# Decoder layer on one core: queries and keys projected apart, scores as plain fp32 products on the two 64-row halves, loop reordered

## What is computed

```python
# x: 8 x 256 x 128, context: 8 x 512 x 128, fp32
x = x + attn(layernorm(x))        # rmsnorm * scale; 16 heads of 64; softmax(q k^T / 8) v; w_out, b_out
x = x + xattn(ctx, layernorm(x))  # one head of 128, 512 context rows, biases on q, v and output
x = x + ffn(layernorm(x))         # 128 -> 512 -> 128, relu, activations and weights quantised to 8 bit
```

```python
q = jnp.einsum('bsd,dhe->bshe', h, wq)
k = jnp.einsum('bsd,dhe->bshe', h, wk)
...
weights = jnp.einsum('bqhd,bkhd->bhqk', q, kf)
```

## Time and profile before

| | |
|---|---|
| runs | 435.38, 437.57, 438.6 us, median 437.57 |
| span of the profiled execution | 435.1 us |
| its own time | not listed apart; the three runs are from 0.3 to 3.5 us above this span |
| busy: TensorE, weight loads | 402.7 us (93%), 333.1 us (77%) |
| busy: VectorE, ScalarE, GpSimd | 322.4 us (74%), 262.0 us (60%), 161.5 us (37%) |
| chain that ended last | TensorE 65%, VectorE 18%, issue 8%, ScalarE 6% |

### The profile page before, as it was taken

One profiled execution on the slowest core, in us unless ns is written; L12 is line 12 of the kernel. 1 busy time (PEld: TensorE's weight loads), 2 busy tenths in 40 slices (PEclk: granted clock), 3 DMA queues, 4 the chain that ended last, 5 costly groups with the idle time before them and its releaser, 6 DMA issues.

```text
span 435.1 us, 9030 instructions
## 1 busy us (share of the span) xinstructions
PE 402.7 (93%) x2981; PEld 333.1 (77%) x2981; DVE 322.4 (74%) x780; ACT 262.0 (60%) x808; POOL 161.5 (37%) x177
## 2 busy tenths in 40 slices
PE   3889999999999999999999999999999999998646
PEld 3787888788878887888888887898788888866115
DVE  2677767866897489867886689748976779757883
ACT  2576665665566565575566556665566565825672
POOL 1055334542454344542454245434454244421000
PEclk9899999999999999999999999999999999999668
DMA  7400000000100010001000010001000000000003
GB/s 232 130 2 2 0 2 2 2 2 2 36 2 3 2 36 0 0 0 36 0 0 0 2 34 0 0 0 36 0 0 0 24 2 2 1 2 0 0 0 98
DMA packets 11878, 7.50 MB, mean 17 GB/s; under 512 B 1232, under 2 KB 11216, under 8 KB 11856
## 3 DMA queue, kind: packets, MB, share of 16 engines
q1 hardware_dynamic: 11568, 6.69, 5.2%
q10 hardware_dynamic: 288, 0.52, 0.4%
HBM read 6.16 MB, written 1.05 MB: 17 GB/s over the span
## 4 chain that ended last, share of the span: by engine, by line
PE 65%; DVE 18%; issue 8%; ACT 6%; DMA 1%; POOL 1%; DVEq 0%; POOLq 0%; ACTq 0%
PE o_bank L467 11%; PE pT L458 9%; PE acc_bank L474 7%; DVE negmax L897 5%; PE score L437 5%; PE score L435 5%; PE score L436 5%; ACT prob L731 4%; PE side_bank L435 3%; PE q_bank L435 2%; PE q_bank L437 2%; PE side_bank L437 2%; PE q_bank L436 2%; PE side_bank L436 2%; PE side_bank L512 2%
## 5 line engine op out<-in xcount | busy, mean ns | idle before, releaser
L1249 POOL TENSOR_TENSOR prob<-prob,rinv 128x512 f32<-128x512 f32 x128 | 133.0, 1042 | 200.6 <-DVE rinv L901 196.8
L731 ACT ACTIVATE prob<-score,negmax 128x256 f32<-128x256 f32 x256 | 118.9, 470 | 103.3 <-DVE negmax L897 103.2
L897 DVE TENSOR_REDUCE negmax<-score 128x2 f32<-128x512 f32 x128 | 87.6, 685 | 51.3 <-PE score L437 50.4
L904 DVE COPY pT<-pT 128x512 f32<-128x512 f32 x128 | 86.4, 677 | 0.0
L458 PE MATMUL pT<-ident,prob 128*128 128x128 f32 x512 | 76.6, 272 | 0.0
L435 PE MATMUL score<-ht_hi,q_hi 128*128 128x256 f32 x256 | 75.0, 293 | 0.0
L437 PE MATMUL score<-ht_hi,q_lo 128*128 128x256 f32 x256 | 72.0, 281 | 0.0
L436 PE MATMUL score<-ht_lo,q_hi 128*128 128x256 f32 x256 | 71.7, 280 | 0.0
L467 PE MATMUL o_bank<-pT,v_sb 128*64 128x256 f32 x512 | 69.4, 392 | 0.0
L458 PEld LDWEIGHTS pT<-ident,prob 128*128 128x128 f32 x512 | 58.9, 141 | 0.4 <-issue 0.4
L474 PEld LDWEIGHTS acc_bank<-wo_sb,oT 128*128 128x128 f32 x256 | 33.4, 190 | 24.3 <-issue 24.2
(11 more groups left out here) (209 smaller groups left out, 600.3 us busy)
## 6 DMA issues: line engine op xcount, KB each, us to landing
c_sb<-in_ctx_dram SPq DMA_DIRECT2D x8, 256.0 KB, 2.9
x_sb<-in_x_dram SPq DMA_DIRECT2D x8, 128.0 KB, 2.8
out_dram<-xn_all SPq DMA_DIRECT2D x4, 256.0 KB, 2.3
big<-in_L_attn_wk_dram ACTq DMA_DIRECT2D x1, 512.0 KB, 3.9
big<-in_L_attn_wq_dram SPq DMA_DIRECT2D x1, 512.0 KB, 6.1
big<-in_L_attn_wv_dram SPq DMA_DIRECT2D x1, 512.0 KB, 6.9
wo_sb<-in_L_attn_w_out_dram SPq DMA_DIRECT2D x1, 512.0 KB, 6.7
w_sb<-in_L_ffn_w_dram SPq DMA_DIRECT2D x2, 256.0 KB, 4.6
```

Of the source, the lines that this page charges most:

```text
L731: last = nc.scalar.activation(prob[:, slot, t, :], score_bank[r][:, t * S:(t + 1) * S], ACT.Exp, bias=negmax[:, slot, t:t + 1], scale=1.0, ...
L897: nc.vector.tensor_reduce(negmax[:, slot], score_bank[r][:].rearrange("p (t k) -> p t k", k=S), X_AXIS, ALU.max, negate=True).then_inc(max ...
L904: nc.vector.tensor_copy(pT[:, slot].rearrange("p k q -> p (k q)"), pT_bank[r][:]).then_inc(pT_done, 1)
L1249: nc.gpsimd.tensor_tensor(prob[:, slot], prob[:, slot], rinv[:, slot].unsqueeze(2).to_broadcast([P, QT, S]), ALU.mult).then_inc(prob_done, 1)
```

## The change

The weights of queries and keys are no longer multiplied together. They are split as they were loaded (`wqk_hi`, `wqk_lo`), without transposes. `project_qk` projects the queries of a pair's two heads (rows 0 to 63 and 64 to 127) and its keys, again in six passes of 256 columns. ScalarE copies both to `qk_sb` as plain fp32; nothing is split. The scores are four plain fp32 matmuls of 64 rows for a pair, which alternate between the row halves and between the two score banks.

The loop's order changes on all engines: scores of both heads stand together, after the side task of the first place; the side task of the second place stands ahead of the output projection, and that ahead of the values. V1 and V3 become W1 and W3, made in steps 0 and 1 of the batch that uses them; UX is made in two halves. VectorE inverts the sums of the second head at the start of the next step, and makes the low part of TH ahead of the residual.

```diff
-PLACE = {(0, 0): "TC", (1, 1): "TH", (2, 0): "V0", (2, 1): "TX", (3, 0): "QX", (3, 1): "SX0",
-         (4, 0): "SX1", (4, 1): "PX0", (5, 0): "PX1", (5, 1): "UX", (6, 0): "OX", (6, 1): "V1",
-         (7, 0): "V2", (7, 1): "V3"}
+PLACE = {(0, 0): "TC", (0, 1): "W1", (1, 0): "W3", (1, 1): "TH", (2, 0): "V0", (2, 1): "TX", (3, 0): "QX",
+         (3, 1): "SX0", (4, 0): "SX1", (4, 1): "PX0", (5, 0): "PX1", (5, 1): "UX0", (6, 0): "UX1", (6, 1): "OX",
+         (7, 0): "V2"}
 PAIRS_PER_BATCH = 8
-PREPARE = ["TH", "V0", "V1", "V2", "V3"]
-LAST_PLACE = {k: t for k, t in PLACE.items() if t not in PREPARE}
+PREPARE = ["TH", "V0", "V2"]
+OWN = ["W1", "W3"]
+AFTER_LAST = ["UX0", "UX1", "OX"]
+LAST_PLACE = {k: t for k, t in PLACE.items() if t not in [*PREPARE, *AFTER_LAST]}
 LAST_PLACE[6, 1] = "TL"
-LAST_PLACE[PAIRS_PER_BATCH, 0] = LAST_PLACE.pop((5, 1))
-LAST_PLACE[PAIRS_PER_BATCH, 1] = LAST_PLACE.pop((6, 0))
-PLACES = {"first": {k: t for k, t in PLACE.items() if t in PREPARE}, "mid": PLACE, "last": LAST_PLACE}
...
-            def project_q(pair, hp):
-                for r in range(2):
-                    a = (slice(None), pair // 4, r, pair % 4)
-                    last = three_passes(q_bank[:, r * S:(r + 1) * S], a_hi[a], a_lo[a], ht_hi[:, hp], ht_lo[:, hp])
+            def project_qk(pair, hp):
+                for n in range(2):
+                    last = three_passes(q_bank[:, n * S:(n + 1) * S], wqk_hi[:, n, pair, :], wqk_lo[:, n, pair, :],
+                                        ht_hi[:, hp], ht_lo[:, hp])
                 last.then_inc(q_raw, 1)
-            def scores(r, parity, hp):
+            def scores(parity):
                 for t in range(QT):
-                    q = (slice(None), parity, r, slice(t * P, (t + 1) * P))
-                    last = three_passes(score_bank[r][:, t * S:(t + 1) * S], q_hi[q], q_lo[q],
-                                        ht_hi[:, hp], ht_lo[:, hp])
-                last.then_inc(score_raw, 1)
+                    for r in range(2):
+                        rows = slice(r * E, (r + 1) * E)
+                        last = nc.tensor.matmul(score_bank[r][:, t * S:(t + 1) * S],
+                                                qk_sb[rows, parity, 0, t * P:(t + 1) * P], qk_sb[rows, parity, 1, :],
+                                                start=True, stop=True)
+                        if t == QT - 1:
+                            last.then_inc(score_raw, 1)
...
                 more_q, more_scores = ahead(kind, j, 3), ahead(kind, j, 2)
-                hp = parity if j < PAIRS - 2 else 1 - parity
                 if more_scores:
-                    pe.wait_ge(q_lo_done, g + 3)
+                    pe.wait_ge(qk_done, g + 3)
                 if more_q:
-                    project_q((j + 3) % PAIRS, parity if j < PAIRS - 3 else 1 - parity)
-                if more_scores:
-                    pe.wait_ge(exp_done, 2 * g + 3)
-                    scores(0, j % 2, hp)
-                pe.wait_ge(prob_done, 2 * g + 1)
-                wait(pe, pT_done, 2 * g - 1)
-                turn_probs(0, 2 * j % 8)
+                    project_qk((j + 3) % PAIRS, parity if j < PAIRS - 3 else 1 - parity)
                 if task := side_at(kind, j, 0):
                     side(kind, b, 1 - parity, i, task)
                 if more_scores:
                     pe.wait_ge(exp_done, 2 * g + 4)
-                    scores(1, j % 2, hp)
+                    scores(j % 2)
+                pe.wait_ge(prob_done, 2 * g + 1)
+                wait(pe, pT_done, 2 * g - 1)
+                turn_probs(0, 2 * j % 8)
                 pe.wait_ge(prob_done, 2 * g + 2)
                 wait(pe, pT_done, 2 * g)
                 turn_probs(1, 2 * j % 8 + 1)
+                if task := side_at(kind, j, 1):
+                    side(kind, b, 1 - parity, i, task)
                 if not (kind == "first" and j < 1):
-                    if j == 1:
-                        pe.wait_ge(side_free, side_before(kind, b))
                     wait(pe, o_done, g - 1)
-                    slot = 2 * (j - 1) % 4
-                    values((j - 1) % PAIRS, (slot, slot + 1), 1 - parity if j == 0 else parity)
                 if not (kind == "first" and j < 2):
                     if j == 2:
                         wait(pe, x1_done, b)
                     project_out((j - 2) % PAIRS)
-                if task := side_at(kind, j, 1):
-                    side(kind, b, 1 - parity, i, task)
+                if not (kind == "first" and j < 1):
+                    if j == 1:
+                        pe.wait_ge(side_free, side_before(kind, b))
+                    slot = 2 * (j - 1) % 4
+                    values((j - 1) % PAIRS, (slot, slot + 1), 1 - parity if j == 0 else parity)
...
             pe.wait_ge(side_free, 1)
-            pe.wait_ge(a_done, 2)
-            project_q(0, 0)
+            pe.wait_ge(wqk_lo_done, 2)
+            project_qk(0, 0)
...
             def step(kind, b, parity, i, j):
                 g = b * PAIRS + j
                 more_scores = ahead(kind, j, 2)
                 if ahead(kind, j, 3):
                     act.wait_ge(q_raw, g + 4)
-                    split_hi((j + 3) % 2)
+                    keep_qk((j + 3) % 2)
+                if task := side_at(kind, j, 0):
+                    side(kind, b, 1 - parity, task)
                 if more_scores:
                     act.wait_ge(max_done, 2 * g + 5)
                     exps(0, (2 * j + 4) % 8)
-                if task := side_at(kind, j, 0):
+                if task := side_at(kind, j, 1):
                     side(kind, b, 1 - parity, task)
                 if more_scores:
                     act.wait_ge(max_done, 2 * g + 6)
...
+            def weights_hi(n, half):
+                copy(wqk_hi[:, n, 4 * half:4 * half + 4, :],
+                     (wq_sb, wk_sb)[n][:, half * 512:half * 512 + 512].rearrange("p (j d) -> p j d", d=P),
+                     scale=(ASCALE, 1.0)[n]).then_inc(wqk_hi_done, 1)
+            act.wait_ge(load_wk, 16)
+            weights_hi(1, 0)
+            act.wait_ge(load_wq, 16)
+            weights_hi(0, 0)
             act.wait_ge(load_scale, 16)
             side("start", -1, 0, "TH")
...
                 more_scores = ahead(kind, j, 2)
+                if ahead(kind, j, 1):
+                    dve.wait_ge(exp_done, 2 * g + 4)
+                    invert_sums((2 * j + 3) % 8)
+                if kind == "mid" and j == PAIRS - 1:
+                    aggregate(2, b, *PLAIN_NORM)
                 if prepare and j == 0:
                     dve.wait_ge(load_x[1 - parity], (i + 2) * 16)
                     statistics(0, tiles(x_sb[:, 1 - parity]), b + 2)
+                if cross and j == 2:
+                    normalise(1, tiles(xn2), tiles(x1_sb), b, xn2_done)
+                if task := side_at(kind, j, 0):
+                    side(kind, b, 1 - parity, task)
                 if more_scores:
-                    dve.wait_ge(score_raw, 2 * g + 5)
-                    maxima(0, (2 * j + 4) % 8)
+                    for r in range(2):
+                        dve.wait_ge(score_raw, 2 * g + 5 + r)
+                        maxima(r, (2 * j + 4 + r) % 8)
+                early = side_at(kind, j, 1) == "SX0"
+                if early:
+                    side(kind, b, 1 - parity, "SX0")
                 if prepare and j == 0:
                     aggregate(0, b + 2, *FIRST_NORM)
-                if cross and j == 2:
-                    aggregate(1, b, *PLAIN_NORM)
                 dve.wait_ge(pT_raw, 2 * g + 1)
                 keep_turned(0, 2 * j % 4)
-                if ahead(kind, j, 3):
-                    dve.wait_ge(q_hi_done, g + 4)
-                    split_lo((j + 3) % 2)
                 if kind == "mid" and j == PAIRS - 1:
                     cross_norm(b)
-                if task := side_at(kind, j, 0):
-                    side(kind, b, 1 - parity, task)
-                if kind == "mid" and j == PAIRS - 2:
-                    dve.wait_ge(side_free, side_index(kind, b, "OX") + 1)
-                if more_scores:
-                    dve.wait_ge(score_raw, 2 * g + 6)
-                    maxima(1, (2 * j + 5) % 8)
-                if cross and j == 2:
-                    normalise(1, tiles(xn2), tiles(x1_sb), b, xn2_done)
-                if kind == "mid" and j == PAIRS - 2:
-                    statistics(2, x2_of(b), b)
                 if more_scores:
                     dve.wait_ge(exp_done, 2 * g + 5)
                     invert_sums((2 * j + 4) % 8)
+                if (task := side_at(kind, j, 1)) and not early:
+                    side(kind, b, 1 - parity, task)
+                if cross and j == 1:
+                    residual(b, 1 - parity)
                 if kind == "mid" and j == PAIRS - 2:
-                    aggregate(2, b, *PLAIN_NORM)
+                    dve.wait_ge(side_free, side_index(kind, b, "OX") + 1)
                 dve.wait_ge(pT_raw, 2 * g + 2)
```

(17 more changed lines are left out.)

151 lines of the change are left out of this document (49 added, 102 removed).

## The result

The changed kernel takes 418.39 us (median of four runs, 417.8 to 419.88) beside 437.1 of the kernel before in the same comparison: ratio 0.958, 95% interval 0.955 to 0.961. The forecast was 418. The profiled execution of the changed kernel took 418.03 us, with a span of 416.2 (before: 435.1).

What follows compares the result with a forecast made beforehand. TensorE's own stream was taken as the bound. Mid batches -11.7, first batch -2.3, last batch +0.2 and start -5.5 sum to -19.3 us: from the median 437.57 to 418, range 403 to 437.

Steps and rivals of the forecast that it cites:

- The score block: Scores in each step: four row-half matmuls take 1.21 us for 1.41, -0.20 us a pair, 62 pairs, -12.4 us.
- Cheap switching: Rival on the scores: array drains for only one load, block costs 0.95 us, total 402 us; chance 0.20.
- no overlap: Rival on the scores: row halves run one after the other, block 2.05 us against 1.41, total 471 us; chance 0.07.
- The hole at V0: First V half's wait for the low part of the turned input: closes, -1.0 us a batch, bounds -1.0 and 0.
- New waits: Late inputs after the reordering, mainly scores of steps 2 and 3: +0.55 us a batch, bounds 0 to 1.5.
- VectorE's relief pays nothing: Projection: VectorE loses one 128x512 subtraction a pair, which pays nothing by itself since VectorE is not the bound.
- Middle batch: Each of six mid batches in the loop: -1.6 - 1.0 + 0.55 + 0.1 = -1.95 us, together -11.7.
- First: First batch: -1.6, its hole -1.0, +0.3 for scores waiting for exponentials while the pipeline fills: -2.3 us.
- Last and tail: Last batch: six pairs -1.2, two V halves moved in +1.4, so +0.2 us; tail nothing, at most 0.5.
- The start: Before the loop: first projection at 9.2 us, loop at 20.5 instead of 26.0, -5.5 us (-7.3 to -3).

Runs made afterwards that it cites:

- one-pass scores: Changed kernel with queries and keys kept rounded as fp32r, so each score matmul is one pass of lower precision: 386.66 us.
- GpSimd's wait: Changed kernel, but in step 1 GpSimd waits for VectorE's cross norm scaling (`xn2`) before scaling the second head's probabilities: 413.78 us.
- six profiles with the same start: Profiles of six follow-up kernels with the changed kernel's start or nearly so, each profiled once; second step began at 26.5 to 27.7 us including the warmed-start kernel's.

## Why the prediction was right, and where it was not

- **The score block**, -0.20 us a pair: right. Plain steps give 0.22, the block is 1.20 for the forecast 1.21, and its parts are as named: streaming 0.84 by overlapping halves, the rest switching. Cheap switching is ruled out by the step of 3.83 us with one-pass scores, and no overlap by the time line; what no overlap would cost was forecast at +0.84 and measured at +0.86. That it would come out as 12.4 us of the total was too much: taken alone in the new loop it was worth 8.1. From the old scores to the new ones with GpSimd's wait it is 12.7 (426.45 to 413.78), of which up to 0.7 may be the wait's own, since old scores with the wait were not run.
- **The hole at V0**, -1.0 a batch: right in size, and the chain forecast fits the trace: with S the end of step 1's scores (2.6 us into the step), the low part ends at S+2.8 for the forecast S+2.85, and V0 runs at S+3.6 for S+3.5. Neither reason given is the whole: the work between grew by 0.5 us, not enough alone; VectorE's order gave 0.73; and the 0.43 of ScalarE's new order were in the chain but not named as a reason.
- **New waits**, +0.55: the size was near (0.71), by luck, since the place and the mechanism were not those forecast. The forecast had step 3's scores wait for a bank and step 4's for the low part of QX; neither waits, as the score lines show one wait in all, of 1.8 us, in the first step. I had the scaling behind the root as 0.60 us from the tail's copy of that chain, where GpSimd has nothing else to do, and I followed it to the maxima and not to TX, the task that needs `xn2`. With 0.60 TX would not have waited, as GpSimd's wait showed.
- **VectorE's relief pays nothing**: not quite. The same work put back costs 3.6 us, in the step of TX and the one behind it.
- **Middle batch** -1.95: -2.1, which is 8 x 0.22 and 1.0 less, 0.71 more. **First** -2.3: -2.6. **Last and tail** +0.2: +0.4. The cost of the split UX was not measured apart.
- **The start**, -5.5: -4.1 in the one profile. The first projection came at 9.60 for 9.2. I took 2 us for a low clock; until about 17.2 us every pass took 0.213. It also had 0.80 us between starts at 10.8, waiting for the cross weights' transfer. The six profiles with the same start put the loop at 20.5 to 21.3 for this one's 21.9 and the forecast's 20.5, so how much the term missed is not settled. The fall of the clock after a wait, in three of the six, was not among my reasons at all. And the mean of 0.93 over the old start counts the time ahead of its first clock record, at 10.2 us, as full speed.

In these two profiles the terms' errors (+1.4 at the start, -1.2 in the first seven batches) nearly cancel, so that the total came nearer than its parts is luck.

## What to carry to other kernels

A block of matmuls in another shape of tile cost about 0.36 us here for coming and going, so it pays when it saves more streaming than that, and two such blocks side by side share one change; but look first at what the moved block was covering. For a hole, compare two lengths, the work that TensorE has between and the chain over the other engines, and see which of them the change moved. When a hole closes or TensorE's stream gets shorter, follow each chain of VectorE and GpSimd to the next TensorE task that needs it, with durations taken from a place where the other engine is busy too. At the start, judge the clock by the distance of the starts of like matmuls, ask what the next wait will do to it, and look at several profiles before a difference of 1 us is believed.

## What was not expected of the hardware

- VectorE's scaling of 128 x 128 takes 0.34 us alone and 1.05 when it starts with GpSimd's scaling of 128 x 512, and it ends with it. The tiny `veps` of 128 x 2 behind the statistics is held likewise in six batches (0.97 us for 0.17). The maxima (0.68), the copies (0.68) and the statistics (0.28) are not stretched by GpSimd.
- Row halves overlap without alternation: 4.46 us a step in either order of four matmuls.
- The granted clock read 1.00 for 7.8 us in which matmuls ran at half speed, because the trace had no record of it there. And the same wait of 1.83 us was followed by a clock at its low level for some 3.5 us in some profiles and not in others with the same start; what decides it stays open.
